# A fused LoRA, router and expert kernel: slot list from bf16 digits, and the residual added in DRAM by accumulating transfers

## The reference

```python
c = x @ W.T + b + 2 * ((x @ A[slot]) @ B[slot])          # LoRA of rank 16, one adapter per sequence
scores = softmax(c @ router_w + router_b) + router_bias   # 16 experts in 4 groups
# keep the 2 best groups, in them the 2 best experts; their scores are the gates
y = sum over the 2 experts of gate * ((silu(c @ w1 + b1) * (c @ w2 + b2)) @ w3 + b3)
z = (silu(c @ sw1 + sb1) * (c @ sw2 + sb2)) @ sw3 + sb3   # shared expert, inner width 256
out = x + y + z
```

## Time and profile before

| quantity | value |
|---|---|
| three timed runs | 152.08, 152.35, 152.58 us |
| profiled execution, own time | 152.1 us |
| its span on the core | 150.3 us |
| what lies around the span | 1.8 us |
| PE busy | 142.7 us, 95% |
| DVE, ACT, POOL busy | 90.9, 70.6, 53.0 us |
| granted TensorE clock, mean | 0.999 of full speed (2.4 GHz) |
| moved by DMA | 41.09 MB, mean 273 GB/s |

### The profile page before, as it was taken

The page is one execution under the profiler, slowest core; times in us unless marked ns, Lnnn a source line. Parts: engine busy times, 40 slices in busy tenths (PEclk is TensorE's granted clock), DMA queues, the critical chain, the costliest instruction groups (busy, mean ns, idle before and its releaser), DMA issues.

```text
span 150.3 us, 3119 instructions
## 1 busy us (share of the span) xinstructions
PE 142.7 (95%) x990; PEld 112.3 (75%) x991; DVE 90.9 (60%) x230; ACT 70.6 (47%) x138; POOL 53.0 (35%) x68
## 2 busy tenths in 40 slices
PE   7969999999978999999999999999999999999991
PEld 7747676776755877888898887888778887688760
DVE  1683556355997959998853545663333223499992
ACT  3561274366633646018596665566556665300000
POOL 7570211000000020135542767667575666350000
PEclk9999999999999999999999999999999999999999
DMA  4979999999994999911653356876788999786963
GB/s 143 345 239 336 415 394 404 339 382 413 417 412 158 289 388 369 391 48 39 190 141 125 99 184 190 298 227 246 265 286 236 368 400 324 227 325 197 293 253 140
DMA packets 16767, 41.09 MB, mean 273 GB/s; under 512 B 2448, under 2 KB 2448, under 8 KB 16624
## 3 DMA queue, kind: packets, MB, share of 16 engines
q1 hardware_dynamic: 11488, 23.33, 43.5%
q0 software_dynamic: 3776, 12.59, 25.0%
q10 hardware_dynamic: 1488, 4.98, 9.0%
HBM read 31.98 MB, written 8.91 MB: 272 GB/s over the span
## 4 chain that ended last, share of the span: by engine, by line
PE 77%; DVE 7%; DMA 5%; ACT 3%; issue 3%; POOL 2%; POOLq 0%; DVEq 0%
PE bank L1024 28%; PE bank L1222 21%; PE bank L1233 10%; DMA lora_raw<-in_lora,lora_row 5%; PE bank L1207 5%; PE bank L1080 2%; PE bank L1303 2%; PE bank L1090 2%; DVE xt_ring L746 1%; PE bank L1297 1%; PE bank L1099 1%; PE bank L1197 1%; ACT xtT_h L539 1%; PE bank L1057 1%; DVE xT_l L715 1%
## 5 line engine op out<-in xcount | busy, mean ns | idle before, releaser
L1222 PE MATMUL bank<-xgT_sb,w_now 128*128 128x128 f32 x288 | 35.2, 275 | 0.0
L1222 PEld LDWEIGHTS bank<-xgT_sb,w_now 128*128 128x128 f32 x288 | 33.6, 192 | 0.6 <-issue 0.5
L469 POOL DMA_INDIRECT xg_sb<-xt_rows,slot_tok x22 | 21.4, 971 | 12.7 <-issue 5.5
L475 POOL DMA_INDIRECT y_rows<-y_ring,slot_row x18 | 19.3, 1070 | 15.3 <-DVE y_ring L930 15.0
L922 DVE SCALAR_TENSOR_TENSOR hT_sb<-bank,b_now,glT_sb 128x128 f32<-128x128 f32 x18 | 6.3, 351 | 25.3 <-ACT glT_sb L636 22.7
L626 ACT COPY w_now<-w_sb 128x1024 f32 x18 | 18.9, 1048 | 0.8 <-issue 0.8
L618 ACT COPY xgT_sb<-bank 128x512 f32<-128x512 f32 x18 | 10.5, 585 | 18.5 <-PE bank L1207 18.5
L1233 PE MATMUL bank<-w_sb,hT_sb 128*128 x36 | 18.3, 593 | 0.0
L930 DVE COPY y_ring<-bank 128x512 f32<-128x512 f32 x18 | 12.4, 691 | 6.8 <-PE bank L1233 6.8
L1207 PEld LDWEIGHTS bank<-ident,xg_sb 128*128 128x128 f32 x72 | 8.9, 141 | 8.0 <-issue 7.9
L1024 PE MATMUL bank<-condW_h,xT_h 128*128 128x512 f32 x31 | 13.4, 433 | 1.3 <-DVE xT_l L715 1.2
(11 more groups left out here) (178 smaller groups left out, 247.2 us busy)
## 6 DMA issues: line engine op xcount, KB each, us to landing
w_sb<-in_w SPq DMA_DIRECT2D x8, 1024.0 KB, 9.6
w_sb<-in_w ACTq DMA_DIRECT2D x2, 2048.0 KB, 13.8
low_sb<-y_rows SPq DMA_DIRECT2D x8, 512.0 KB, 5.8
xt_rows<-xt_ring SPq DMA_DIRECT2D x8, 256.0 KB, 5.4
x_sb<-in_x SPq DMA_DIRECT2D x8, 256.0 KB, 2.9
out<-x_sb SPq DMA_DIRECT2D x8, 256.0 KB, 3.4
xT_raw<-in_xT SPq DMA_DIRECT2D x3, 512.0 KB, 7.0
sw_raw<-in_sw SPq DMA_DIRECT2D x1, 1024.0 KB, 8.7
```

Of the source, the lines that this page charges most:

```text
L469: pool.indirect_dma_start(xg_sb[:, b % 4, :], None, xt_rows, bass.IndirectOffsetOnAxis(ap=slot_tok[:, b:b + 1], axis=0)).then_inc(gathered ...
L475: pool.indirect_dma_start(y_rows, bass.IndirectOffsetOnAxis(ap=slot_row[:, b:b + 1], axis=0), y_place(b), None).then_inc(y_scattered[b % Y ...
L1222: mm = pe.matmul(half[:, 0:P], w12_now[:, s % 2, (2 * k + m) * INTER:(2 * k + m + 1) * INTER], xgT_sb[:, s % 2, k, :], start=(k == 0), sto ...
```

## The change

1. **Slot list.** `onehot_off`, `blk_hit` and `blk_tok` become bf16. The pair's number is held as two digits (tile and partition), so `blk_tok` has 2 x 32 columns and each of the sixteen matmuls 64 columns in place of 32. DVE makes the first digit and ACT the second; POOL's multiplication goes. DVE joins the digits with one more instruction.
2. **End.** SP copies x to the output in DRAM during stage 3, where it loaded `x_sb`. ACT starts each tile's sum: `acc` = gate x lower row, for all eight tiles. DVE adds the higher row and the shared expert's bank. POOL adds the finished tile onto x in DRAM by a transfer that accumulates. The diagonal matmuls go.
3. **Order.** ACT's `hi_lhT` stands ahead of `exps`, and DVE's `mask_lh` ahead of `shift_logits` for pairs 0 and 1; `lo_xtT(3)` moves behind them. POOL waits with four constants until `condW_done` is full. On DVE the expert numbers (`eid`) come ahead of the gates and `hidden(2)`. ACT takes the weights of block 0 ahead of `gate_silu(3)`, makes `hi_hs(2)` later, and loads one more register (`low_at`); PE loads one less.

```diff
 # SP
-                sp.dma_start(x_sb[:, i, :], x[i * P:(i + 1) * P, :]).then_inc(x_in, 16)
+                sp.dma_start(out[i * P:(i + 1) * P, :], x[i * P:(i + 1) * P, :]).then_inc(x_in, 16)
...
-            for n in range(TILES):
-                sp.wait_ge(acc_done, n + 1)
-                sp.dma_start(out[n * P:(n + 1) * P, :], x_sb[:, n, :]).then_inc(out_stored, 16)
             sp.wait_ge(out_stored, 16 * TILES)
 # POOL
             gather_lora(1)
+            pool.wait_ge(condW_done, KC)
             pool.affine_select(out=tmp[:], in_=tmp[:], compare_op=ALU.not_equal, fill=1.0, base=0,
...
-            pool.wait_ge(blk_hit_ready, 1)
-            pool.tensor_tensor(blk_tok[:], blk_hit[:], pair_row[:].unsqueeze(2).to_broadcast(by_block), ALU.mult
-                               ).then_inc(blk_tok_ready, 1)
...
+            pool.wait_ge(x_in, 16 * TILES)
+            for i in range(TILES):
+                pool.wait_ge(acc_done, i + 1)
+                pool.dma_start(out[i * P:(i + 1) * P, :], acc[:, i, :], accum_op=ALU.add).then_inc(out_stored, 16)
 # ACT
-            for u in range(3):
-                gate_silu(u)
+            gate_silu(0)
+            gate_silu(1)
+            act.wait_ge(blk_hit_ready, 1)
+            act.activation(blk_tok[:, :, 1, :], blk_hit[:], ACT.Copy, scale=part_f[:, 0:1]).then_inc(blk_tok_ready, 1)
+            gate_silu(2)
...
-            for n, i in enumerate(LOW_ON_PE):
-                act.activation(diag[:, n, :], ident[:], ACT.Copy, scale=val[:, 0, i:i + 1]).then_inc(diag_ready, 1)
+            act.wait_ge(low_in, 16 * TILES // 2)
+            for i in range(TILES):
+                act.activation(acc[:, i, :], low_tiles(first, i), ACT.Copy, scale=val[:, 0, i:i + 1]).then_inc(low_scaled, 1)
 # DVE
+            dve.wait_ge(blk_hit_ready, 1)
+            dve.tensor_tensor(blk_tok[:, :, 0, :], blk_hit[:], tile_digit[:].unsqueeze(2).to_broadcast([P, NJ, BPAD]), ALU.mult
+                              ).then_inc(blk_tok_ready, 1)
...
-            then(dve.tensor_copy(slot_pair[:], bank[6][:, 0:BPAD]))
+            then(dve.tensor_scalar(slot_high[:], bank[6][:, 0:BPAD], float(P), None, ALU.mult))
+            then(dve.tensor_tensor(slot_pair[:], slot_high[:], bank[6][:, BPAD:2 * BPAD], ALU.add))
...
+            def add_high(i):
+                dve.wait_ge(high_in[i // 2], 16)
+                dve.wait_ge(low_scaled, i + 1)
+                add(i, dve.scalar_tensor_tensor(out=acc[:, i, :], in0=low_tiles(first, TILES + i), scalar=val[:, 1, i:i + 1],
+                                                in1=acc[:, i, :], op0=ALU.mult, op1=ALU.add))
             def add_shared(i):
                 dve.wait_ge(shared_done, i + 1)
-                dve.tensor_tensor(x_sb[:, i, :], x_sb[:, i, :], shared_bank(i)[:], ALU.add).then_inc(acc_done, 1)
+                dve.wait_ge(dve_step, added[i])
+                dve.tensor_tensor(acc[:, i, :], acc[:, i, :], shared_bank(i)[:], ALU.add).then_inc(acc_done, 1)
...
             add_high(0)
-            add_shared(0)
-            add_low(1)
             add_high(1)
-            add_shared(1)
...
+            for i in range(TILES):
+                add_shared(i)
+                if i + 2 < TILES:
+                    add_high(i + 2)
 # PE
-            pe.wait_ge(blk_tok_ready, 1)
+            pe.wait_ge(blk_tok_ready, 2)
...
-                mm = pe.matmul(bank[6][:, 0:BPAD], onehot_off[:, j, :], blk_tok[:, j, :],
+                mm = pe.matmul(bank[6][:, 0:2 * BPAD], onehot_off[:, j, :], blk_tok[:, j].rearrange("p d b -> p (d b)"),
...
-                if i in LOW_ON_PE:
-                    n = LOW_ON_PE.index(i)
-                    pe.wait_ge(diag_ready, n + 1)
-                    pe.wait_ge(low_in, 16 * TILES // 2)
-                    mm = pe.matmul(shared_bank(i)[:], diag[:, n, :], low_tiles(first, i), start=False, stop=True)
```

More of the change, by code:

```diff
@@ L37 @@
 WARM_UP = 10
-LOW_ON_PE = (5, 6, 7)
 STACK = 96
@@ L569, in _ @@
                     hi_lora(g)
+                if i % 2 == 1 and g < GROUPS_L:
+                    hi_lhT(g)
                 if i in (3, 5, 7):
                     exps((i - 3) // 2)
-                if i % 2 == 1 and g < GROUPS_L:
-                    hi_lhT(g)
                 hi_xtT(i)
@@ L648, in _ @@
             act.wait_ge(sh_up_done, IC)
[L649 to L652, removed]
+            e = expert_of(0)
+            take_w12(0, 0, e)
+            take_b12(0, 0, e)
+            gate_silu(3)
+            e = expert_of(1)
+            take_w12(1, 1, e)
+            take_b12(1, 1, e)
             act.wait_ge(sh_up_done, 2 * IC)
@@ L659, in _ @@
             silu(0, 0)
+            hi_hs(2)
             hi_hs(3)
@@ L662, in _ @@
             left = blocks_left(act)
+            act.wait_ge(low_known, 1)
+            first = low_at(act)
             def group(b):
@@ L794, in _ @@
             then(dve.tensor_copy(slot_no[:], slot_no_i[:]))
-            then(dve.tensor_scalar(pair_row[:], slot_no[:, 0:K * TILES], float(-K * T), None, ALU.add))
+            then(dve.tensor_copy(part_f[:], part_i[:]))
+            then(dve.tensor_scalar(tile_digit[:], cols[:, 0:K * TILES], float(TILES), None, ALU.add))
+            then(dve.tensor_scalar(slot_no_pad[:], slot_no[:], float(K * T + T), None, ALU.add))
             lo_lora(0)
@@ L809, in _ @@
                     add_cond(i + 1)
-                if i in (3, 5, 7):
-                    shift_logits((i - 3) // 2)
+                if i == TILES - 1:
+                    shift_logits(PAIRS - 2)
                 if i in (4, 6):
@@ L818, in _ @@
                     mask_lh(g)
+                if i in (3, 5):
+                    shift_logits((i - 3) // 2)
+                if i == 5:
+                    lo_xtT(3)
                 if i % 2 == 0 and g + 2 < XCHUNKS:
                     lo_xT(g + 2)
-                if i >= 1:
+                if i >= 1 and i != 4:
                     lo_xtT(i - 1)
@@ L892, in _ @@
             dve.engine_nop().then_inc(eid_ready, 1)
-            then(dve.tensor_scalar(slot_f32, slot_pair[:], float(K * T), None, ALU.add))
+            dve.wait_ge(gate_ones, 2)
+            twice = gate[:, :, 0:64].rearrange("p i (m c) -> p i m c", m=2)[:, :, :, 0:E].bitcast(F32R)
+            then(dve.tensor_copy(twice, sc[:].unsqueeze(2).to_broadcast([P, TILES, 2, E])))
+            dve.tensor_tensor(gate[:, :, 64:64 + E].bitcast(F32R), sc[:], gate[:, :, 0:E], ALU.subtract).then_inc(gate_ready, 1)
+            hidden(2)
+            then(dve.tensor_scalar(slot_f32, slot_pair[:], float(-T), None, ALU.add))
             then(dve.tensor_scalar(slot_empty, slot_pair[:], 0.0, None, ALU.is_equal))
-            then(dve.tensor_tensor(slot_empty, slot_empty, slot_no[:], ALU.mult))
+            then(dve.tensor_tensor(slot_empty, slot_empty, slot_no_pad[:], ALU.mult))
             then(dve.tensor_tensor(slot_row[:], slot_f32, slot_empty, ALU.add))
@@ L1260, in _ @@
                     left = blocks_left(pe)
-                if b == 2:
-                    pe.wait_ge(low_known, 1)
-                    first = low_at(pe)
             def group(b):
@@ L1296, in _ @@
                             [part[:, c, :] for part in sw3_split], start=(c == 0), stop=False)
-                mm = pe.matmul(shared_bank(i)[:], gateT[:, i * P:(i + 1) * P], b3s_split[:], start=False,
-                               stop=(i not in LOW_ON_PE))
-                if i in LOW_ON_PE:
-                    n = LOW_ON_PE.index(i)
-                    pe.wait_ge(diag_ready, n + 1)
-                    pe.wait_ge(low_in, 16 * TILES // 2)
-                    mm = pe.matmul(shared_bank(i)[:], diag[:, n, :], low_tiles(first, i), start=False, stop=True)
-                mm.then_inc(shared_done, 1)
+                pe.matmul(shared_bank(i)[:], gateT[:, i * P:(i + 1) * P], b3s_split[:], start=False, stop=True
+                          ).then_inc(shared_done, 1)
 def kernel(x, itok_B_0_23, L0_cond_W, L0_cond_b, L0_cond_lora_As, L0_cond_lora_Bs, L0_ffn_router_w,
```

53 lines of the change are left out of this document (14 added, 39 removed).

## The result

The changed kernel took 158.94 us (median of 4 runs, 157.79 to 160.16) beside 152.47 us for the kernel before. The ratio is 1.040, with a 95% interval of 1.034 to 1.047. Forecast was 151.2 us, so it was wrong in sign. The profiled execution took 158.76 us, its span is 157.0 (150.3 before).

A forecast was written before the change was run, and what follows sets the result against it. PE was taken to bound the kernel (busy 142.7 of 150.3 us). Terms 0 + 0.3 + 0.8 + 0 + 2.3 - 2.25 gave 1.15 us of gain, 152.35 to 151.2 us; 8-in-10 range 149.5 to 153.5.

The forecast's parts named there:

- POOL's constants: Near 9 us, constants waiting for `condW_done`: gain 0, between 0 and 0.1, since PE next waits for the adapter rows.
- Order of stage 1: ACT's and DVE's reordering brings `cond_lora(3)` forward, against a delay at `exps(0)`: gain 0.3 us, bounds -0.2 and 0.95.
- Slot list: Sixteen bf16 matmuls save PE 1.1 us, less 0.3 for ACT's extra work: net gain 0.8, bounds 0.2 and 1.2.
- Stage 3: Expert blocks stay PE-bound and copies of x replace loads: gain 0, bounds -0.3 and 0.1.
- The end up to the last addition: Last higher load lands at 142.3, DVE's last addition ends at 145.55 against 147.8: gain 2.3 us, bounds 1.7 and 2.7.
- rival E: The end keeps its length because the higher load comes as late as 144.5: 153.5 us; chance 0.22 together with B.
- B: Rival: accumulating transfers land late after each `acc_done`, making the kernel slower, 153.5 or 154.2 us; chance 0.22 together with E.
- The end from the last addition on: POOL's queue, accumulating transfer and last waits take 4.75 us against 2.5 before: 2.25 dearer, bounds 1.0 and 4.6.
- from last addition to POOL's issue: Behind DVE's last addition: 0.65 us of POOL's issuing queue plus 0.1.
- issue to landing: POOL's last accumulating transfer: 2.9 us as for the best scatters, plus 0.6 for accumulating.
- landing to the end of the span: Last waits behind the final landing: 0.5 us, as before with SP's store.
- The sum: Whole kernel: all terms together gain 1.15 us, 150.95 us for the profiled execution and 151.2 for the median.

The follow-up runs named there:

- e1: The changed kernel with the end of the kernel before (x loaded into `x_sb`, diagonal matmuls, SP's plain stores): 151.33 us, ratio 0.9939.
- e9: The kernel before with only the bf16 slot list and its order at the start of stage 3, order of stage 1 unchanged: ratio 0.9955.
- after: The changed kernel itself, with all parts of the change, against the kernel before: 158.94 us, ratio 1.040.
- e8: e1 with the eight copies of x to the output added beside the loads of x: ratio 1.0033.
- e2: The changed kernel with POOL's eight transfers at the end storing plainly, x left out of the sum: 154.33 us, ratio 1.0127.
- e13: e2 without the copies of x to the output, x left out of the sum: 152.84 us, ratio 0.9997.
- e3: The changed kernel with only tile 7's transfer accumulating, the others plain, x left out of those: 155.66 us in one run.
- e14: The changed kernel with SP storing the eight tiles plainly, x copied but left out of the sum: 151.5 us, ratio 0.9851.
- e11: e1 without diagonal matmuls; for tiles 3 to 7 ACT scales lower rows and POOL adds them onto x in SBUF: ratio 1.0196.

## Why the prediction was wrong, step by step

**POOL's constants, 0.** Right. PE's wait near 9 us fell to 0.7, and the adapter rows took it back.

**Order of stage 1, 0.3.** Right in mechanism. PE waited 0.65 before the fifth tile's turn (forecast 0.5) and 0.49 before `cond_lora(3)` (forecast 1.1) where it had been 1.42: 0.2 net. e1 and e9 differ by 0.2.

**Slot list, 0.8.** Nearly right: 1.17 came off the matmuls (forecast 1.1), `onehot_off` took 1218 ns twice, as forecast from the earlier trace rows, and ACT took back 0.6 and not 0.3. The front was forecast at 1.1 and gave 0.9 by e1.

**Stage 3, 0 with bounds -0.3 and 0.1.** Wrong as to the copies of x. I compared them with the loads that they replace and looked only at PE's gathers. They delay the loads of rows instead: the fourth lower one took 14.3 us in after (9.6 before), the first higher one 10.0 (5.5). It is so in each trace that has these landings: 14.3 to 16.3 and 9.9 to 10.2 with copies, 9.6 to 11.7 and 5.2 to 5.6 with loads of x. The price is 1.4 us when the copies stand beside the loads (e8), and against no traffic of x at all 2.0 by the ratios or 0.5 by the spans (e2 and e13); what a copy costs in place of a load no run shows. Nor do the runs show how a copy delays a load issued at 124.1, when the last copy had landed at 116.6.

**The end up to the last addition, 2.3.** Wrong by 3.0: forecast 144.5, measured 147.53. PE and the number of instructions were right. From the last load's landing to the end of the five instructions it took 3.3 us (forecast 3.25). What failed is the load itself: I let it be issued 1.1 us earlier, with the front, and land in 4.6. It was issued at 137.8, not earlier at all, since the last scatter, issued 0.7 us earlier, took 5.3 us to land in place of 4.5; and it took 6.4. In e2, where the stores are plain, it was issued at 137.7 and took 5.1. So of the 3.0 us some 1.3 are the accumulating transfers of tiles 0 to 4, issued before it landed; 1.1 are the late issue, in e2 too, and 0.5 the landing that I had too short. This is rival E. Its place was right and its size nearly (144.5 on the clock of before, 143.4 with the front's gain; measured 144.2); I gave it and B together 0.22.

**The end from the last addition on, -2.25.** This is the step that failed most: 4.75 us forecast, 9.5 measured. Its terms:

| term | forecast | measured |
|---|---|---|
| from last addition to POOL's issue | 0.75 | 0.3 |
| issue to landing | 3.5 | 6.8 |
| landing to the end of the span | 0.5 | 2.4 |

A lone one landed in 4.2 (e3): a plain store of POOL 2.6 where I had taken 2.9, and the addition 1.6 where I had taken 0.6. That is 0.7 of the 3.3 us. The other 2.6 are the transfers ahead, at 2.0 us each. I had counted POOL's queue for issuing and not that of the DMA engines. By my own numbers they were already near their limit (0.63 + 0.6 us a tile, a tile every 1.3 us, loads beside them); at 2.0 us a tile they fall behind with each. By bytes the last six slices had room, but the engines move such bytes at a third of the rate. The last 1.9 us I took from SP's stores, with no bound. The trace of before had a row for it, which I didn't read: POOL's DRAIN, which ended 1.9 us behind the landing of its last scatter.

The Trainium skill, "Collectives: The Full Stack", "The bandwidth ceiling: the fold count and why AG ≠ RS ≠ AR", has a reducing transfer at half the rate. The trace agrees in direction and goes further: 130 against 378 GB/s for a full share, about a third. I had applied it to one tile and not to eight in a row. Its "DMA: Bandwidth & Descriptors", "Latency and other measured facts", has GpSimd's first byte 0.4 us behind SyncE's; the traces agree roughly: plain stores with little beside them land in 2.3 us from POOL (e2) and 2.0 from SP.

**The sum.** Span forecast 149.15, measured 157.0, so 7.85: 3.1 up to the last addition, 4.7 behind it. B's sign was right, but its size (154.2 at most) was too small by the queue, the ending and the late load.

## What to carry to other kernels

Price a transfer at the end of a kernel as a stream: its time of the DMA engines against the rate at which tiles are finished, and what else is then loaded. Count the way from its landing to the end of the program by the engine that issues it; that engine's DRAIN in an earlier trace gives it. Bulk copies that nobody waits for still delay the small loads that somebody waits for, and a move on one engine is only half an edit if its consumer's place on the other stays.

## What the runs showed of the hardware

- An accumulating transfer of 256 KB from SBUF to DRAM took 1.8 to 2.0 us of all 16 DMA engines, a plain one of POOL 0.6 to 0.8 (after, e2, e14). POOL needed 0.86 us to issue the one and 0.54 for the other.
- A program whose last transfer was POOL's ended 2.4 to 2.8 us behind its landing (ten versions), since POOL's DRAIN ended 2.2 to 2.6 behind it; with SP's last it ended 0.4 behind.
- The last load of rows (512 KB) landed 6.4 to 8.4 us after its issue beside accumulating transfers (five versions), 3.6 to 6.0 beside plain ones (thirteen).
- A DVE instruction with two SBUF inputs stood still for 6.2 us while POOL ran five additions in SBUF (e11).
- The kernel before itself took 152.3 to 152.6 us beside most versions and 157.7 and 159.3 beside others.
